# Mamba-2 block and FFN on one core: the sum of squares of the gated norm leaves TensorE

## The reference, cut to what matters

```python
y = _ssd(hs, A, Bm, Cm, D, dt, dt_bias).reshape(b, l, INTER)
g = y * jax.nn.silu(gate)
gg = g.reshape(b, l, G, GS)
var = jnp.mean(gg * gg, axis=-1, keepdims=True)
g = (gg * jax.lax.rsqrt(var + EPS)).reshape(b, l, INTER) * norm_w
return g @ out_w.T
```

## Time and profile before

| | |
|---|---|
| runs | 1739.31, 1740.41, 1741.37 us; median 1740.41 |
| span of the profiled execution, first to last instruction | 1737.2 us |
| around the span | the profiled execution has no time of its own beside its span; the median is 3.2 us above it |
| busy | PE 99%, weight loads 83%, DVE 70%, ACT 69%, POOL 68% |
| granted clock | 0.999 of full, mean |
| DMA | 209.87 MB on SP's queue, 41.7% of 16 engines' span |

### The profile page before, as it was taken

One profiled execution on the slowest core, in us unless ns is written; L12 is line 12 of the kernel. 1 busy time (PEld: TensorE's weight loads), 2 busy tenths in 40 slices (PEclk: granted clock), 3 DMA queues, 4 the chain that ended last, 5 costly groups with the idle time before them and its releaser, 6 DMA issues.

```text
span 1737.2 us, 27735 instructions
## 1 busy us (share of the span) xinstructions
PE 1724.5 (99%) x9925; PEld 1436.9 (83%) x9925; DVE 1221.0 (70%) x2154; ACT 1192.8 (69%) x2232; POOL 1182.1 (68%) x1058
## 2 busy tenths in 40 slices
PE   9999999999999999999999999999999999999999
PEld 7788888888888888888888888888888888787887
DVE  8886778768785769676875878586867688663323
ACT  6887677767867677767776777768777777663421
POOL 5586768677777668676867687766867686774510
PEclk9999999999999999999999999999999999999999
DMA  5534435343543443443534354345343353444201
GB/s 192 171 107 116 125 116 169 109 119 105 162 128 114 121 146 112 121 116 112 174 115 115 97 162 128 114 122 151 114 118 113 110 174 101 118 114 134 80 15 49
DMA packets 122056, 211.63 MB, mean 122 GB/s; under 512 B 24256, under 2 KB 28992, under 8 KB 121920
## 3 DMA queue, kind: packets, MB, share of 16 engines
q1 hardware_dynamic: 121920, 209.87, 41.7%
HBM read 205.09 MB, written 4.72 MB: 121 GB/s over the span
## 4 chain that ended last, share of the span: by engine, by line
PE 97%; DVE 1%; DMA 1%; POOL 0%; ACT 0%; issue 0%; POOLq 0%
PE bank L1712 19%; PE bank L1714 18%; PE bank L1713 18%; PE bank L1788 7%; PE bank L1846 7%; PE bank L1836 7%; PE bank L1829 7%; PE bank L1803 5%; PE bank L1762 2%; PE bank L2091 1%; PE bank L2092 1%; PE bank L2093 1%; PE bank L1862 1%; PE bank L1772 1%; PE bank L1953 1%; DMA w_raw<-in_wp 0%
## 5 line engine op out<-in xcount | busy, mean ns | idle before, releaser
L704 POOL TENSOR_TENSOR w_l<-w_raw,w_h 128x512 fp32r<-128x512 f32 x288 | 379.6, 1321 | 341.2 <-ACT w_h L900 341.2
L1712 PE MATMUL bank<-x_h,w_h 128*128 128x512 f32 (+1 forms) x1328 | 527.0, 397 | 3.9 <-DVE x_ch L1385 2.3
L1714 PE MATMUL bank<-x_h,w_l 128*128 128x512 f32 (+1 forms) x1328 | 519.7, 391 | 0.0
L1713 PE MATMUL bank<-x_l,w_h 128*128 128x512 f32 (+1 forms) x1328 | 518.1, 390 | 0.0
L1385 DVE SCALAR_TENSOR_TENSOR x_ch<-bank,par,x_ch 128x511 f32<-128x511 f32 (+2 forms) x384 | 287.2, 749 | 80.3 <-ACT x_ch L918 71.2
L953 ACT ACTIVATE decay<-decay,cols 128x128 f32<-128x128 f32 x1024 | 318.2, 390 | 3.7 <-DMA cdec<-cdec_scratch 1.6
L1712 PEld LDWEIGHTS bank<-x_h,w_h 128*128 128x128 f32 (+1 forms) x1328 | 249.5, 188 | 55.1 <-issue 3.1
L1714 PEld LDWEIGHTS bank<-x_h,w_l 128*128 128x128 f32 (+1 forms) x1328 | 249.2, 188 | 54.6
L1713 PEld LDWEIGHTS bank<-x_l,w_h 128*128 128x128 f32 (+1 forms) x1328 | 249.7, 188 | 51.1
L1415 DVE TENSOR_TENSOR decay<-decay,bank 128x512 f32<-128x512 f32 x256 | 171.3, 683 | 107.1 <-ACT decay L953 107.1
L918 ACT ACTIVATE x_ch<-bank,par 128x512 f32<-128x512 f32 x128 | 99.0, 774 | 185.6 <-PE bank L1714 185.5
(11 more groups left out here) (161 smaller groups left out, 2760.0 us busy)
## 6 DMA issues: line engine op xcount, KB each, us to landing
w_raw<-in_wp SPq DMA_DIRECT2D x288, 256.0 KB, 3.0
decay<-cum_scratch SPq DMA_DIRECT2D x256, 256.0 KB, 4.1
ec<-ecum_scratch SPq DMA_DIRECT2D x96, 256.0 KB, 6.2
ow_raw<-in_ow SPq DMA_DIRECT2D x64, 256.0 KB, 4.8
w_raw<-in_w SPq DMA_DIRECT2D x48, 256.0 KB, 2.7
acc<-in_x SPq DMA_DIRECT2D x8, 256.0 KB, 4.5
out<-acc SPq DMA_DIRECT2D x8, 256.0 KB, 2.0
cols<-cols_scratch SPq DMA_DIRECT2D x16, 96.0 KB, 2.7
```

Of the source, the lines that this page charges most:

```text
L704: pool.tensor_tensor(w_l[:, s, :], w_raw[:, s, :], w_h[:, s, :].bitcast(F32), ALU.subtract).then_inc(wl_ready, 1)
L1712: pe.matmul(dst, wh, xh, start=(opens and k == 0), stop=False)
L1713: pe.matmul(dst, wh, xl, start=False, stop=False)
L1714: last = pe.matmul(dst, wl, xh, start=False, stop=(k == len(terms) - 1 and not more))
```

## The change

PE no longer makes the sum over the 128 partitions. DVE transposes `y[:, 0, :]`, which turns each 32x32 block in place, and reduces over 32 columns: four partial sums on each partition, for a token of each of four blocks. They are stored to a small DRAM scratch (128 x 4 floats, two of them in turn), and four DMAs of 32 partitions x 4 single floats bring them back so that each token's four partial sums lie on its own partition. `mean_square` reduces these and adds EPS. On SP the store stands behind the second decay load, the fetch behind the first weight load; on DVE `turn_squares` stands ahead of `fade`, and `mean_square` moves from before `gated` to after it. The waits of `match` and `new_state` on the spare columns go, and ACT's wait for `ss_done` becomes one for `sq_summed`.

```diff
+            def store_squares(g, k):
+                K = g * CHUNKS + k
+                sp.wait_ge(sq_summed, K + 1)
+                sp.dma_start(sq_dram[K % 2], sq_part[:, :]).then_inc(sq_stored, 16)
+            def fetch_squares(g, k):
+                K = g * CHUNKS + k
+                sp.wait_ge(sq_stored, 16 * (K + 1))
+                if some(K):
+                    sp.wait_ge(mean_ready, K)
+                src = sq_dram[K % 2].rearrange("(c t) b -> b t c", c=QUADS)
+                for q in range(QUADS):
+                    sp.dma_start(sq_full[q * SQ:(q + 1) * SQ, :], src[q], allow_slow_non_contiguous=True).then_inc(sq_fetched, 16)
...
             def last_chunk(k):
+                if k == CHUNKS - 1:
+                    store_squares(LAST, k - 1)
+                    fetch_squares(LAST, k - 1)
                         load_decay(LAST, k + 1, q)
+                        if q == 1 and k > SC:
+                            store_squares(LAST, k - 1)
                     load_ec(LAST, k + 1)
+                    if k > SC:
+                        fetch_squares(LAST, k - 1)
...
                     sp.wait_ge(in_done, KEND * QUARTERS)
+                    store_squares(LAST, k)
+                    fetch_squares(LAST, k)
...
                             load_decay(gn, kn, q)
+                            if q == 1 and some(K):
+                                store_squares(*before)
...
                     if not first:
+                        fetch_squares(*before)
+                    if not first:
                         load_next_w(g, last, b, tiles[0])
...
                         first_up()
+                        store_squares(g, k)
+                        fetch_squares(g, k)
...
             def mean_square(g, k):
                 K = g * CHUNKS + k
-                dve.wait_ge(ss_done, K + 1)
-                dve.tensor_scalar(mean_sq[:, :], total_of(K), EPS, None, ALU.add).then_inc(mean_ready, 1)
+                dve.wait_ge(sq_fetched, 16 * QUADS * (K + 1))
+                dve.tensor_reduce(mean_sq[:, :], sq_full[:, :], mybir.AxisListType.X, ALU.add).then_inc(mean_step, 1)
+                dve.wait_ge(mean_step, K + 1)
+                dve.tensor_scalar(mean_sq[:, :], mean_sq[:, :], EPS, None, ALU.add).then_inc(mean_ready, 1)
+            def turn_squares(g, k):
+                K = g * CHUNKS + k
+                dve.wait_ge(sum_ready, K + 1)
+                dve.transpose(y[:, 1, :], y[:, 0, :]).then_inc(sq_turned, 1)
+                dve.wait_ge(sq_turned, K + 1)
+                if some(K):
+                    dve.wait_ge(sq_stored, 16 * K)
+                dve.tensor_reduce(sq_part[:, :], y[:, 1, :].rearrange("p (b t) -> p b t", b=QUADS),
+                                  mybir.AxisListType.X, ALU.add).then_inc(sq_summed, 1)
...
+                    if not first:
+                        turn_squares(*before)
                     if k != 1:
                         fade(g, k)
...
                         add_state(g, k)
+                        gated(g, k)
                         mean_square(*before)
-                        gated(g, k)
...
-            def square_total(g, k):
-                K = g * CHUNKS + k
-                pe.wait_ge(sum_ready, K + 1)
-                if K == MIDDLE:
-                    pe.wait_ge(xdt_ready, K + 2)
-                pe.matmul(total_of(K), y[:, 0, :], ones[:, :], start=True, stop=True).then_inc(ss_done, 1)
...
                     inside(g, k)
-                    if not first:
-                        square_total(*((g, k - 1) if k else (g - 1, CHUNKS - 1)))
                     new_state(g, k)
```

More of the change, by code:

```diff
@@ L33 @@
 PIECE = KT * P
+SQ = 32
+QUADS = P // SQ
 SLOT_TILES = [[("g", 0), ("g", 1), ("c", 0), ("c", 1), ("g", 2)],
@@ L129, in build @@
     cols_dram = nc.dram_tensor("cols_scratch", (GROUPS, BATCH, P, UNIT_COLS), F32, kind="Internal").ap()
+    sq_dram = nc.dram_tensor("sq_scratch", (2, P, QUADS), F32, kind="Internal").ap()
     cdec_dram = nc.dram_tensor("cdec_scratch", (BATCH, GROUPS, GH * SC), F32, kind="Internal").ap()
@@ L149, in build @@
         mean_sq, rstd = sb("mean_sq", [P, 1]), sb("rstd", [P, 1])
-        sb("align", [P, 112])
+        sq_part, sq_full = sb("sq_part", [P, QUADS]), sb("sq_full", [P, QUADS])
+        sb("align", [P, 104])
         scan_ctx = ExitStack()
@@ L260, in build @@
         MIDDLE = (GROUPS - 1) * CHUNKS + SC - 1
-        def total_of(K):
-            return xt[1][:, 0:1] if K == MIDDLE else cbb[:, 2 * P:2 * P + 1]
         def normed(k, c, squares, gates):
@@ L330, in build @@
         out_done = sem("out_done")
-        ss_done = sem("ss_done")
+        sq_turned = sem("sq_turned")
+        sq_summed = sem("sq_summed")
+        sq_stored = sem("sq_stored")
+        sq_fetched = sem("sq_fetched")
+        mean_step = sem("mean_step")
         decay_seen = sem("decay_seen")
@@ L623, in body @@
                     more, gn, kn = next_chunk(last, g, k)
+                    before = (g, k - 1) if k else (g - 1, CHUNKS - 1)
                     if last and b == 1:
@@ L977, in square @@
                 if some(K):
-                    act.wait_ge(ss_done, K)
+                    act.wait_ge(sq_summed, K)
                 act.activation(y[:, :, :], sgT[:, b, :, tok(c)], ACT.Square, scale=GCH ** -0.5).then_inc(sq_ready, 1)
@@ L1260, in _ @@
             act.wait_ge(out_done, 2 * KEND)
-            act.wait_ge(ss_done, KEND)
+            act.wait_ge(sq_summed, KEND)
             for m in range(FT):
@@ L1579, in last_chunk @@
                     return
+                turn_squares(LAST, k - 1)
                 gate_up(pairs[0] - 1)
@@ L1583, in last_chunk @@
                 add_state(LAST, k)
+                gated(LAST, k)
                 mean_square(LAST, k - 1)
-                gated(LAST, k)
                 if k < CHUNKS - 1:
@@ L1593, in last_chunk @@
                 norm_apply(1, k - 1)
+                if k == CHUNKS - 1:
+                    turn_squares(LAST, k)
                 if k < CHUNKS - 1:
@@ L1648, in body @@
                         norm_apply(1, 2)
+                        turn_squares(g, k)
                         for q in range(QUARTERS):
@@ L1768, in match @@
                     pe.wait_ge(s_ready, K * QUARTERS)
-                if some(K - 1):
-                    pe.wait_ge(mean_ready, K - 1)
                 pe.transpose(cbb[:, P:2 * P].bitcast(F32R), bcTr[:, b, 0, tok(c)], ident_r[:, :])
@@ L1816, in new_state @@
                     pe.wait_ge(x_l_ready, CHUNKS + k - 1)
-                if K == MIDDLE + 1:
-                    pe.wait_ge(mean_ready, K)
                 for h in range(2):
@@ L1962, in last_chunk @@
                 inside(LAST, k)
-                if k > SC:
-                    square_total(LAST, k - 1)
                 new_state(LAST, k)
@@ L2003, in last_chunk @@
                     out_half(LAST, k, 1)
-                    square_total(LAST, k)
                     up(t + 4)
@@ L2051, in body @@
                             norm_transpose(1, 2)
-                            square_total(g, k)
                         out_half(g, k, 1)
@@ L2073, in _ @@
             pe.wait_ge(lora2_l_ready, 2)
-            pe.wait_ge(mean_ready, KEND)
             pe.wait_ge(acc_ready, KEND)
```

## The result

Each experiment below was timed beside the kernel before on its own chip (1737.9 to 1739.2 us, medians); "ratio" is to that, with its 95% interval.

The account below looks back on a forecast made before the run. PE was taken to bound the kernel, carrying 97% of the chain of waits. Stalls summed over the groups to 146 us, on the 1737.2 us span with 3.2 us around it: 1886 us, range 1800 to 2000.

Parts of the forecast that it names:

- The gain, 14 us: On PE behind `inside`: without the sum of squares the next matmul starts 0.22 us sooner in each of 64 chunks.
- Rival E: PE's 0.22 us comes back as another gap behind `inside`, and the fetch is early: 1740 us, chance 0.03.
- DVE's pair, small reduce, SP's issues: Added work: transpose and reduce 0.55 us, small reduce with add 0.35, five SP issues at 0.43; alone costing PE nothing.
- When the fetch lands: In SP's queue: behind the weight load, not before 889.5; four fetches at 0.37 us plus the store, 1.8 us more.
- the prediction's other estimate: Cost of the four fetches by element, from the skill's transpose figures: 0.8 us instead of 1.5.
- 0.3 for the store: In the fetch's landing time: the store to scratch adds 0.3 us, within the 1.8 us in all.
- What PE sees: PE's delay by chunk: 6.4 us in 0, 4.5 in 1, 2.8 in 2, 5, 6; 146 us in all.
- Rival C: Small packets are dear, or the clock falls: 1950 to 2004 us, say 1975; chance 0.17.
- The clock: PE idling 2 to 6 us may halve its clock: 1.7 us lost three times a group, 41 us, as bound only.
- D: The fetch does not queue, landing before about 888.5 in chunks 2, 5, 6: faster, 1726 us; chance 0.07.
- the highest bound worked out: Fetch packets at 3.1 us give 1963 us; 41 us of clock loss on top gives 2004.
- A: The forecast itself: the fetch lands behind the queue and DVE is blocked; 1886 us (1850 to 1930), chance 0.60.

Follow-up runs that it names:

- the shift: The kernel before with its `align` tensor 8 columns longer, so all tensors behind it start 32 bytes later while x_h and x_l stay: 1760.5 us, ratio 1.013.
- experiment 1: Two kernels from the changed one: store and fetches left out, 1748.3 us; or both kept and DVE not waiting for the fetched values, 1751.8 us.
- fetch_decay4: The changed kernel with the four fetches alone moved behind the fourth decay load, ahead of ec and the weight: 1843.3 us, ratio 1.059.
- sp_early: The changed kernel with the store behind the first decay load and the fetches behind the second: 1805.3 us, ratio 1.038.

## Why the prediction was wrong, step by step

- **The gain, 14 us.** Right in place (0.26 us behind `inside`) and a little too large (10.8 us measured, 0.17 a chunk and not 0.22), but the layout took 21: by the rows of the shift, (533.1 + 525.5 + 525.4) - (527.0 + 519.7 + 518.1) = 19 us in the projections and 2 in the output products. No step of mine looked at the allocation. Rival E, a gap elsewhere that eats the gain, had the fact and not the cause.
- **DVE's pair, small reduce, SP's issues.** Right, and nothing waits for them.
- **When the fetch lands.** Right in order, too early by 1.3 us in chunks 2, 5, 6: 12.1 forecast, 13.4 in the mean. The fetches cost 0.8 us behind the weight (1.5 in the chunk shown), not above my 1.5; the prediction's other estimate, 0.8 us by element, came out nearer. The order isn't strict: the first of the four fetches is in 0.7 us before the weight in the chunk shown, so "it cannot land before 889.5" is true only of the last one, for which DVE waits and which comes at least 0.65 us behind all loads ahead of it in each of the 55 chunks of groups 0 to 6. The failed term is "0.3 for the store". The two kernels of experiment 1 differ by the transfers alone: without them the fourth decay load lands at 7.7 us and the weight at 10.5, with them at 9.4 and 12.3, of which some 0.5 us are their later issue. Only the store stands ahead of these loads. In equally busy DMA windows less is moved (7 us before, then 8.7 us after, up to the weight's landing):

```profile
882.50:889.50 7.00, 7.00 (x48) 6.16 (x47) 5.42 (x10) 3.36 (x5) 3.88 (x7) 1.00 0.83 246
```
```profile
934.00:942.70 8.70, 8.13 (x50) 6.71 (x48) 2.25 (x4) 3.89 (x6) 2.54 (x3) 1.00 0.84 189
```

- **What PE sees.** So PE idles 4.2 us in chunks 2, 5 and 6 instead of 3.0 (the forecast's 2.8 and the gain), chunk 1's 6.4 instead of 4.7 (fetch in at 15.8, not 13.8). Chunk 0 was over-priced (4.2 idle, 6.6 forecast), chunks 3, 4, 7 under-priced (0.5, 1.5, 1.6 idle for 0 to 0.3). In all the rest of PE's span is 205.6 us longer; the sum had 146 + 14 = 160. Rival C's dear packets gave 237, but for packets that turned out cheap.
- **The clock, the largest miss.** The sum of 1886 held nothing for it: I took its fall for an upper bound and priced there three losses of 1.7 us in a group, 41 us. In the trace the clock falls in or just behind all 30 stalls of 3 us and more, and with 4 of 33 from 1 to 3 us: four times in a group, each time for 5.5 us in the mean, and 68 us are lost. So more stall costs more than itself: fetch_decay4, with no single stall over 2 us from group 0 to 6, has a clock of 0.995 and loses 6 us to it.
- **Account.** Against the kernel without transfers, record by record in the two profiled executions: 202 us more of idle time, 68 us at half clock, and 25 us of delays too short to show as idle (12 of them at the 92 waits, where a record's modelled end hides 0.13 us, and much of the rest ahead of the products with gT_l): 294.8 us. That kernel's own span is 9.3 us above the one before: 18.2 for the layout, less 8.9 for the matmul that is gone. Together 304.1 us. The profiled execution is the longest of the four; the medians differ by 294 us.
- **D** needed the whole fetch to pass the loads. Its last part landed behind the weight in every such chunk, so D is ruled out; only when issued ahead of them (sp_early) is it early.
- **The range** ended at 2000, and the highest bound worked out was 2004; the result lies above both. Nearest to it was C, whose "or the clock falls" came true, but beside A and not in its place.

## What to carry to other kernels

A small transfer through a queue that carries the large loads lands behind what was issued before it, and the wait belongs on an engine's program just ahead of the first use, not ahead of work that others wait for. A stall on a saturated PE has to be priced with the clock: here a chunk with 4.2 us of idle time took 6.5 us longer (32.2 us where 25.75 are needed without the wait). And a new tensor of a few bytes moves all tensors behind it: compare the addresses of the operands before and after, and the mean of one unchanged group of instructions.

## What the runs showed of the hardware that I had not expected

- The start of the weights against the moving tensor is worth over 2% of a projection's pace: from start to start a median of 227 ns at a distance of 149504 bytes (73 x 2048), 232 and 233 ns at 32 and 64 bytes more, and 227 ns again with all tensors 32 bytes on. Other distances were not tried, so which modulus counts is open, and so is whether the weight load or the moving read is held up. The Trainium skill ("SBUF — State Buffer", Operand start alignment) treats start addresses as a matter of what is legal and says that its runs timed nothing.
- With a store of 128 rows of 16 bytes among them (the kernel that doesn't wait), the 256 KB load issued next lands 0.8 us later than in the kernel before, the one after it 1.3 and the weight 1.6, of which 0.3 to 0.4 is their later issue. The mechanism is open.
- PE work that nobody needs can pay: 392 dummy matmuls took 98 us of busy time and the kernel got 44 us faster, since fewer of its own matmuls ran at half clock.
